# Half of each head's probability transfers from ScalarE's queue, with reordered scores, queries and splits around them

## What is computed

```
h = layernorm(x);  n = rmsnorm(h) * ln_weight
q, k, v = n @ w_q.T, ctx @ w_k.T, ctx @ w_v.T              # 32 heads of 128
p = softmax(where(mask, q k^T + position_bias[head], -inf))
x = x + h + concat_heads(p v) @ w_out.T
x = x + layernorm(x) @ W.T + 2 * layernorm(x) @ W_a @ W_b    # W = code table * absmax
```

## Time and profile before

| | |
|---|---|
| median of 3 runs | 841.38 us (840.92 to 841.69) |
| profiled execution | 841.95 us, with a span of 840.1 us |
| TensorE busy | 826.6 us (98%), granted clock 0.996 of full on average |
| VectorE, ScalarE, GpSimd busy | 450.4, 445.8, 537.5 us (54, 53, 64%) |
| chain that ended last, by engine | PE 86%, DVE 5%, ACT 4%, SyncE's queue 3%, DMA 1% |
| transfers pT<-p_blocks | 496, all issued by SyncE, 32 KB each, 1.8 us from issue to landing |

### The profile page before, as it was taken

The page is one execution under the profiler, slowest core; times in us unless marked ns, Lnnn a source line. Parts: engine busy times, 40 slices in busy tenths (PEclk is TensorE's granted clock), DMA queues, the critical chain, the costliest instruction groups (busy, mean ns, idle before and its releaser), DMA issues.

```text
span 840.1 us, 15757 instructions
## 1 busy us (share of the span) xinstructions
PE 826.6 (98%) x4694; PEld 721.4 (86%) x4694; DVE 450.4 (54%) x754; ACT 445.8 (53%) x1297; POOL 537.5 (64%) x556
## 2 busy tenths in 40 slices
PE   9997999999999999999999999999999999999998
PEld 6876888988889888998889888898889888898786
DVE  6783656246553556246562565436562455626683
ACT  5746555364644656264644557446553546437632
POOL 1654778756784668757786577756687567865440
PEclk9998999999999999999999999999999999999999
DMA  8213323123221223113231133112230232311102
GB/s 327 83 42 94 96 71 98 27 68 109 85 69 53 91 66 95 33 62 96 69 97 60 47 110 97 37 53 92 68 97 28 67 97 69 105 42 51 45 13 88
DMA packets 51125, 64.98 MB, mean 77 GB/s; under 512 B 11008, under 2 KB 37248, under 8 KB 50080
## 3 DMA queue, kind: packets, MB, share of 16 engines
q1 hardware_dynamic: 51104, 64.73, 24.7%
HBM read 44.24 MB, written 4.19 MB: 58 GB/s over the span
## 4 chain that ended last, share of the span: by engine, by line
PE 86%; DVE 5%; ACT 4%; SPq 3%; DMA 1%; issue 1%; POOL 0%; ACTq 0%; POOLq 0%; DVEq 0%
PE w_ps L1176 41%; PE o_ps L1176 32%; PE s_ps L1212 6%; PE s_ps L1218 6%; SPq L341 3%; ACT p_blocks L653 2%; ACT p_blocks L604 1%; DVE ctx_lo L893 1%; DMA pT<-p_blocks 1%; DVE stats L899 1%; DVE resid L1015 1%; DVE resid L942 1%; DVE xn_lo L948 1%; PE s_ps L1242 0%; DVE wv_raw L966 0%
## 5 line engine op out<-in xcount | busy, mean ns | idle before, releaser
L497 POOL TENSOR_TENSOR p<-pos_raw,mask_add 128x1024 f32<-128x1024 f32 x32 | 69.6, 2175 | 113.7 <-ACT p_blocks L653 113.5
L532 POOL TENSOR_SCALAR picked<-codes 128x256 f32<-128x256 int32 x112 | 125.4, 1120 | 19.2 <-POOL level L535 15.6
L653 ACT ACTIVATE p_blocks<-p,neg_max 128x128 f32<-128x128 f32 x248 | 96.1, 389 | 57.1 <-DVE neg_max L992 46.5
L535 POOL TENSOR_TENSOR level<-level,picked 128x256 f32<-128x256 f32 x112 | 89.9, 803 | 20.8 <-POOL picked L532 20.8
L469 POOL TENSOR_TENSOR ring_lo<-k_raw,ring_hi 128x256 fp32r<-128x256 f32 x105 | 76.9, 744 | 30.2 <-ACT ring_hi L604 27.2
L604 ACT ACTIVATE ring_hi<-k_raw 128x256 fp32r<-128x256 f32 x105 | 38.7, 412 | 103.3 <-POOL k_raw L459 103.3
L1015 DVE TENSOR_TENSOR resid<-o_ps,resid 128x512 f32<-128x512 f32 x102 | 68.7, 686 | 44.5 <-PE o_ps L1176 44.3
L1176 PE MATMUL w_ps<-ctx_hi,ring_hi 128*128 128x512 f32 x210 | 85.2, 406 | 0.5 <-ACT kT L604 0.5
L1176 PE MATMUL w_ps<-ctx_hi,ring_lo 128*128 128x512 f32 x210 | 82.4, 392 | 0.0
L1176 PE MATMUL w_ps<-ctx_lo,ring_hi 128*128 128x512 f32 x210 | 82.2, 392 | 0.0
L604 ACT ACTIVATE p_blocks<-p_blocks,row_scale 128x128 f32<-128x128 f32 x248 | 77.1, 390 | 1.1 <-DVE row_scale L999 1.1
(11 more groups left out here) (223 smaller groups left out, 2287.9 us busy)
## 6 DMA issues: line engine op xcount, KB each, us to landing
pT<-p_blocks SPq DMA_DIRECT2D x496, 32.0 KB, 1.8
k_raw<-k_dram SPq DMA_DIRECT2D x16, 512.0 KB, 3.3
wv_raw<-wv_dram SPq DMA_DIRECT2D x8, 1024.0 KB, 4.9
q_raw<-q_dram SPq DMA_DIRECT2D x32, 256.0 KB, 3.5
wo_raw<-wo_dram SPq DMA_DIRECT2D x32, 256.0 KB, 3.9
resid<-x_dram SPq DMA_DIRECT2D x2, 1024.0 KB, 12.0
pos_raw<-pos_dram SPq DMA_DIRECT2D x32, 64.0 KB, 3.9
out_dram<-resid SPq DMA_DIRECT2D x8, 256.0 KB, 2.0
```

Of the source, the lines that this page charges most:

```text
L497: pool.tensor_tensor(p[:, :, :], pos, mask_add[:, :, :], ALU.add).then_inc(bias_done, 1)
L532: then(pool.tensor_scalar((level if code == 0 else picked)[:, :], codes[:, :], float(code), NF4[code], match, ALU.mult))
L535: then(pool.tensor_tensor(level[:, :], level[:, :], picked[:, :], ALU.add))
L653: e = act.activation(out(b), p[:, b, :].rearrange("p (k c) -> p k c", c=Q), ACT.Exp, bias=neg_max[:, b:b + 1], accum_out=prob_sum[:, b:b + 1])
```

## The change

Three parts. First, half of the 16 transfers of heads 1 to 30 (keys 2 and 3) are issued by ScalarE, by a new function `move_blocks(h)`, which waits for both turns and stands behind the attention copies and ahead of the drains of the next queries; head 0's 16 stay on SyncE. Second, ahead of the loop: VectorE does head 0's bias and maximum before the split of head 1's query weights and before the last four residuals and the last context split; ScalarE drains head 1's queries between key splits; SyncE loads the first output weights after five context splits in place of eight. Third, TensorE in odd heads makes the first half of the next queries ahead of the attention products instead of behind them, and the scores of head 31 go to another bank, with other waits.

```
@@ last scores
-        last_s = [s_ps[0][:, :, :], w_ps[2][:, :].rearrange("p (b k) -> p b k", b=HB)]
+        last_s = [bank[:, :].rearrange("p (b k) -> p b k", b=HB) for bank in (o_ps[2], w_ps[2])]
@@ SyncE, ahead of the loop and in group()
-            sp.wait_ge(ctx_lo_done, SPLITS)
+            sp.wait_ge(ctx_lo_done, 5)
             load_wo(0, 0)
             load_wo(1, 1)
...
             load_q(3)
+            sp.wait_ge(ctx_lo_done, SPLITS)
...
                         move_blocks((0, 1))
-                        sp.wait_ge(p_turned_done, 2 * h + 2)
-                        move_blocks((2, 3))
@@ ScalarE
+            def move_blocks(h):
+                act.wait_ge(p_turned_done, 2 * h + 2)
+                for k in (2, 3):
+                    for i in range(NQ):
+                        act.dma_start(pT[Q * k:Q * (k + 1), i, :, :],
+                                      p_blocks[Q * i:Q * (i + 1), k, :, :]).then_inc(pT_loaded, 16)
...
-            for p_at in range(2):
-                split_k(1, p_at, key_slot(1, p_at))
+            split_k(1, 0, key_slot(1, 0))
             drain_q(1, 0, next_queries[0])
+            split_k(1, 1, key_slot(1, 1))
+            drain_q(1, 1, next_queries[1])
             for p_at in (2, 3):
                 split_k(1, p_at, key_slot(1, p_at))
-            drain_q(1, 1, next_queries[1])
             split_q(2)
@@ ScalarE, odd_head and even_head, behind the attention copies
+                move_blocks(h)
                 drain_q(h + 1, 0, query_bank(j, 0))
@@ VectorE, ahead of the loop
-            for b in range(HB, B):
-                residual(b)
-            split_first(7, ctx_lo[:, 4, :, :], ctx_sum[3], ctx_hi[:, 4, :, :])
-            split_q(1)
             for hf in range(2):
                 bias_and_max(0, hf)
-            for hf in range(2):
-                scale_rows(0, hf)
+            split_q(1)
+            scale_rows(0, 0)
+            residual(HB)
+            scale_rows(0, 1)
+            for b in range(HB + 1, B):
+                residual(b)
             turn_blocks(0)
+            split_first(7, ctx_lo[:, 4, :, :], ctx_sum[3], ctx_hi[:, 4, :, :])
             split_q(2)
@@ TensorE, odd_head
                 if j == 1:
                     pe.wait_ge(values_added, 2 * ADDS * (g + 1))
+                else:
+                    pe.wait_ge(out_added, B * (2 * g + 1))
+                queries(h + 1, 0, query_bank(j, 0))
                 pe.wait_ge(pT_loaded, 16 * NQ * NQ * h)
...
                 key_product(m, 2, key_slot(j, 2))
-                if j == 3:
-                    pe.wait_ge(out_added, B * (2 * g + 1))
-                queries(h + 1, 0, query_bank(j, 0))
@@ TensorE, behind the loop
-            pe.wait_ge(attn_lo_done, 2 * (H - 2) + 1)
...
-                if b == 3:
-                    pe.wait_ge(biased, 2 * (H - 1) + 2)
+                if b in (2, 3):
+                    pe.wait_ge(biased, 2 * (H - 1) + b - 1)
```

## The result

The changed kernel takes 940.62 us (median of 4 runs, 940.25 to 941.43) against 841.54 for the kernel before: ratio 1.118, interval 1.116 to 1.120, so 99 us slower. The forecast was 900. Its profiled execution took 941.43 us, with a span of 939.6.

What follows compares the result with a forecast made beforehand. TensorE, busy throughout the loop, was taken to bound the kernel, its waits there paid in full. 841.95 - 3.5 + 53.2 + 8.5 = 900.2, less 0.57 to the median: 900; forecast 885 to 915 (0.50), range 862 to 985.

Steps and rivals of the forecast that it cites:

- Ahead of the loop, -3.5: Before the loop: head 0's earlier bias brings head 1's exponentials and the key product forward, -3.5 us.
- Price of an issue, 0.51 + 7 x 0.63: ScalarE's eight issues per head: 0.51 us for the first, 0.63 for each further one as on SyncE, 4.9 us.
- Rival B: Both queues take turns at one generator: 1015 us in all, about 955 at half; whole or in part, chance 0.24.
- Rival A: ScalarE's issues are hidden, under 0.14 us each, so the kernel gets faster: 839 us; chance 0.09.
- Even heads, 14 x 3.8: Loop, 14 even heads: TensorE's fifth output tile waits 3.8 us for VectorE's add behind ScalarE's issues, +53 us.
- Rival C: Each stall in the loop drops TensorE's clock to half, 3.3 us lost each, +46, 946 us in all; chance 0.09.
- Odd heads, 0: Loop, odd heads: TensorE's reordered matmuls and ScalarE's eight issues cost 0, with 2 us in hand.
- None in odd heads: Sign to look for in the loop: no TensorE stall in odd heads.
- Tail, +8.5: Head 30: the last scores wait 5.9 us more behind ScalarE's issues, plus 2.6 for the clock: +8.5 us.

Runs made afterwards that it cites:

- prologue_alone: The changed kernel with all sixteen transfers of a head issued by SyncE and TensorE's old order of odd heads: 837.44 us, ratio 0.9959.
- split_undone: The changed kernel with all 16 transfers of every head back on SyncE, everything else staying changed: 850.87 us, ratio 1.012.
- filled: The changed kernel with 15 matmuls, whose result nobody reads, put into each of the 14 stalls: 914.33 us, ratio 1.087.
- split_alone: The kernel before with the split of the transfers between SyncE and ScalarE and nothing else: 924.86 us, ratio 1.100.
- behind_q: The changed kernel with ScalarE's eight issues of even heads behind both drains and the query split (head 30: behind the drains): 855.18 us, ratio 1.017.
- four_issues: The changed kernel with ScalarE issuing only the four transfers of key 3, SyncE twelve: 875.75 us, ratio 1.042.
- order_back: The changed kernel with TensorE's old order in odd heads, the next queries' first half behind key product 2: 924.7 us, ratio 1.100.
- five_shared: prologue_alone with five of head 0's 16 transfers issued by ScalarE ahead of the loop: 835.23 us, ratio 0.9931.

## Why the prediction was right about the sign and short on the size

The sum as the runs give it: 841.1 - 3.6 (ahead of the loop, prologue_alone) + 13.4 (order of odd heads, split_undone less prologue_alone) + 14 x 3.8 = 53.2 (stalls) + 26.3 (clock behind them, filled) + some 10 (tail: 7.6 us of wait where split_undone has 0.4, and 2.5 behind it, see below) = 940.4. The parts don't simply add in other company: without the new order the split costs 83.8 us (split_alone), beside it 89.8 (split_undone).

**Ahead of the loop, -3.5: right.** Measured -3.6. In the changed kernel head 1's exponentials start at 70.47 (71.2 forecast) and the key product at 77.59 (78.3 forecast), in each case a little sooner than forecast, with 3.20 us of wait ahead of the latter, as the 3.4 foreseen.

**Price of an issue, 0.51 + 7 x 0.63: right.** 5.02 and 5.12 us for eight (4.9 forecast). The page of the changed kernel gives 1.9 us to landing for either queue. Rival B, queues that take turns, fell: with both issuing at once each kept its rate. The Trainium skill (Perfetto Trace Analysis, DMA Instruction — HWDGE) has one generator that is locked for exclusive use; for whole issues of this kernel's two queues the trace doesn't agree, since turns would have made some 10 us of each series, and 5.21 and 5.02 us stand beside each other at 207 to 213. A lock held for a small part of an issue would not show in these rows. The forecast had given that rule 0.24. Rival A, hidden issues, fell by the same rows.

**Even heads, 14 x 3.8: right** in chain, count, releaser and size: 3.57 us of idle and 0.27 of restart.

**Rival C happened, and this is the larger failed step.** The prediction said: "The stall of 3.8 is shorter, so I leave it out", because the row at hand had fallen after 4.76 us of idle. That row says nothing of shorter idle times: in the kernel before, TensorE had no wait between 1.6 and 4.8 us, so both were open. In the changed kernel the clock fell behind each of the 14 stalls of 3.50 to 3.58 us, and behind the 3.20 in head 1; it stayed whole behind 2.21 us (behind_q) and 1.3 (four_issues). It isn't certain at 3.5 either: order_back and split_alone have two stalls of 3.55 each that left it whole. C's price of 3.3 us each came from one long stretch at half clock, 6.8 us; the stretches here were of about 3.4 us, three of them of 6, and 1.9 us was lost on average. The Trainium skill's warning of idle gaps between bursts (TensorE: Matmul & The Clock Gate, Why this matters for your kernels) agrees with the trace of the changed kernel, 0.50 behind each of its 14 stalls, and not with those four of 3.55 us; the forecast cited it and gave it 0.09 only. That C's total, 946, comes out near the 940.6 is luck: its clock is 20 us too dear, and it has nothing for the odd heads.

**Odd heads, 0: the other failed step.** "TensorE's matmuls are the same ones in another order, so by themselves 0." I had followed ScalarE through an odd head, and not asked what the moved queries covered on TensorE itself. They lay between two key products, where a copy on ScalarE has to empty a bank. Without them TensorE idles 0.76 us in each of 14 heads, 10.6 us; with the restarts the order costs 13.4, by split_undone less prologue_alone. "None in odd heads" is what the trace of the changed kernel contradicts first. The part on ScalarE's eight issues there was right: behind_q keeps them at no cost in the loop.

**Tail, +8.5: right** to some 1.5 us. The last scores waited 7.56 us behind ScalarE's issues, where it was 1.37 before, and ran at a lower clock after. These are the two rows of the changed kernel:

```profile
873.42 5.12 ACTq L679 DMA_DIRECT2D pT<-p_blocks  x8
878.59 1.09 ACT L604 ACTIVATE qT<-w_ps 128x512 f32<-128x512 f32 x2 [6.05 <-issue]
```

From the last scores to the end of the span are 939.6 - 879.33 = 60.27 us, and 57.74 in split_undone (849.0 - 791.26): 2.5 us, as the 2.6 taken.

The range held the time only because it reached up for rival B, which did not happen; the missing 26.3 + 13.4 us came from elsewhere.

## What to carry to other kernels

Before a transfer's issue is moved to a computing engine, list what stands behind it in that engine's order and who waits for that: here eight issues took 5 us of ScalarE, which cost nothing in the loop behind the drains, and 5.7 us (3.8 and 1.9) in each of 14 heads ahead of them. When independent work is moved on the bounding engine, look at what waited under it where it was; reordering the same instructions isn't free by itself. And price a stall of a few us on TensorE twice, once as idle and once as clock. That a trace has a stall as long which left the clock whole doesn't clear the next one: 3.55 us of idle left it whole four times in two of these kernels, and 3.5 us brought it down 14 times of 14 in a third.

## What the runs showed of the hardware

Two engines issued transfers at once without slowing each other by more than 0.2 us in eight (5.21 and 5.02 us). Issues on ScalarE ran beside its computing instructions, and ahead of some that stand before them in the code: 62.56 to 63.07 beside the key split of 62.55 in five_shared, and in the changed kernel at 189.14 and 189.70, where the two attention copies that stand ahead of the issues start at 190.11 and 190.59. What the issues held up in these traces is what stands behind them. TensorE's granted clock stayed whole behind idle times of 1.3 and 2.21 us, fell to half behind 3.20 and 3.31, fell behind all 14 of 3.50 to 3.58 in the changed kernel, and stayed whole behind four of 3.55 in order_back and split_alone. Length alone doesn't settle it there; what else does wasn't tried.
